# Second attention rebuilt: head pairs on two row halves, pair-wide maxima and exponentials, x-hat and y's low part on GpSimd, new task orders

## The reference

```
# block 0: one head of 256 channels, scale 1/16
h = film(rmsnorm(x, norm1_w), cond);  Q, K, V = h @ q_w + q_b, h @ k_w + k_b, h @ v_w + v_b
x = x + softmax(Q K^T / 16) V @ proj_w + proj_b
x = x + gelu(film(rmsnorm(x, norm2_w), cond) @ mlp_w1 + mlp_b1) @ mlp_w2 + mlp_b2
# block 1: 16 heads of 16 channels, modulated by six rows of silu(c) @ w_ada + b_ada
xm = layernorm(x) * (1 + scale_msa) + shift_msa
k, q, v = split(xm @ w_qkv, 3);  q = q / 16                 # heads (256, 16, 16)
y = softmax(q k^T over keys) v;  x = x + gate_msa * (y @ w_proj + b_proj)
xm = layernorm(x) * (1 + scale_mlp) + shift_mlp
x = x + gate_mlp * (gelu_tanh(xm @ w_mlp1 + b_mlp1) @ w_mlp2 + b_mlp2)
```

## Time and profile before

| | us |
|---|---|
| median of 3 runs | 1827.96 (1824.01 to 1829.28) |
| span of the profiled execution | 1819.8 |
| median run less that span | 8.2 |
| TensorE busy | 1757.5 (97%) |
| VectorE busy | 1340.7 (74%) |
| ScalarE busy | 944.7 (52%) |
| GpSimd busy | 362.4 (20%) |

### The profile page before, as it was taken

The page is one execution under the profiler, slowest core; times in us unless marked ns, Lnnn a source line. Parts: engine busy times, 40 slices in busy tenths (PEclk is TensorE's granted clock), DMA queues, the critical chain, the costliest instruction groups (busy, mean ns, idle before and its releaser), DMA issues. The chain is left out here.

```text
span 1819.8 us, 46726 instructions
## 1 busy us (share of the span) xinstructions
PE 1757.5 (97%) x15198; PEld 1633.4 (90%) x15198; DVE 1340.7 (74%) x3119; ACT 944.7 (52%) x2099; POOL 362.4 (20%) x470
## 2 busy tenths in 40 slices
PE   7999989999999969999999999999998899999998
PEld 7999989999999967888888888888886899999998
DVE  4888876666666647888888888888885677777776
ACT  2666653333333345777676777777776333333332
POOL 2233331222122200111111111111111212221221
PEclk8999989999999989999999999999999799999999
DMA  7300010000000002111111111111110111111111
GB/s 215 127 20 20 20 33 1 0 0 0 0 0 0 0 14 72 52 49 50 48 48 48 48 48 48 48 48 49 49 49 27 50 47 46 35 46 46 46 42 39
DMA packets 73579, 73.97 MB, mean 41 GB/s; under 512 B 13489, under 2 KB 63985, under 8 KB 73537
## 3 DMA queue, kind: packets, MB, share of 16 engines
q1 hardware_dynamic: 70928, 73.31, 12.9%
q10 hardware_dynamic: 2448, 0.08, 0.1%
q0 software_dynamic: 160, 0.04, 0.0%
HBM read 38.62 MB, written 8.55 MB: 26 GB/s over the span
## 5 line engine op out<-in xcount | busy, mean ns | idle before, releaser
L1418 DVE TENSOR_REDUCE C_negmax<-bank 128x2 f32<-128x512 f32 x512 | 340.2, 686 | 101.1 <-PE bank L1226 98.1
L1338 ACT ACTIVATE C_probs<-bank 128x512 f32<-128x512 f32 x512 | 301.3, 598 | 139.2 <-PE bank L1238 134.4
L1226 PE MATMUL bank<-C_kx,C_qs 128*128 128x256 f32 x1024 | 217.9, 295 | 5.1 <-DMA C_kx<-C_k_hi 2.6
L892 ACT ACTIVATE D_g<-bank,D_bias 128x256 f32<-128x256 f32 x256 | 107.6, 472 | 221.3 <-PE bank L181 221.3
L1238 PE MATMUL bank<-C_qs,C_kx 128*128 128x256 f32 x1024 | 221.2, 298 | 0.1
L892 ACT ACTIVATE B_g<-bank,B_bias 128x256 f32<-128x256 f32 x256 | 107.6, 472 | 218.5 <-PE bank L181 193.1
L1226 PEld LDWEIGHTS bank<-C_kx,C_qs 128*128 128x128 f32 x1024 | 156.2, 189 | 33.3 <-issue 17.7
L1238 PEld LDWEIGHTS bank<-C_qs,C_kx 128*128 128x128 f32 x1024 | 155.9, 189 | 29.0 <-ACT C_probs L1338 15.6
L181 PE MATMUL bank<-D_wt_w_hi,D_g_lo 128*128 128x256 f32 x512 | 147.3, 288 | 6.0 <-DVE D_g_lo L920 4.6
L181 PE MATMUL bank<-B_wt_w_hi,B_g_lo 128*128 128x256 f32 x512 | 145.7, 285 | 5.2 <-DVE B_g_lo L920 5.0
L181 PE MATMUL bank<-B_h_hi,B_wt_w_lo 128*128 128x256 f32 x512 | 147.4, 288 | 1.9 <-DVE B_h_lo L294 1.9
(11 more groups left out here) (265 smaller groups left out, 5218.0 us busy)
## 6 DMA issues: line engine op xcount, KB each, us to landing
C_kx<-C_k_hi SPq DMA_DIRECT2D x256, 64.0 KB, 2.6
C_kx<-C_k_lo SPq DMA_DIRECT2D x128, 64.0 KB, 2.6
C_gbc<-mod_rows SPq DMA_DIRECT2D x32, 256.0 KB, 3.2
D_gbc<-mod_rows SPq DMA_DIRECT2D x32, 256.0 KB, 3.4
out<-xres SPq DMA_DIRECT2D x32, 256.0 KB, 3.5
xres<-in_x SPq DMA_DIRECT2D x4, 1792.0 KB, 16.6
A_orow_bc<-mod_rows SPq DMA_DIRECT2D x32, 128.0 KB, 2.9
stage<-in_L_cond_mlp_w SPq DMA_DIRECT2D x2, 1024.0 KB, 12.5
```

Source lines behind the costliest of these rows:

```text
L892: ins = eng.activation(g[u][:, d * S:(d + 1) * S], hbank[u][:, d * S:(d + 1) * S], func, bias=per_seq(bias1, 2 * u + d, b))
L1226: ins = eng.matmul(sbank[h % 2][:, qh * S:(qh + 1) * S], qs[b.par][:, t * S + qh * P:t * S + (qh + 1) * P], kx[b.par][e][:, t * S:(t + 1) ...
L1338: e_exp.by(eng.activation(probs[h % NP][:, :], stbank[h % 2][:, :], ACT.Exp, scale=scl))
L1418: e_max.by(eng.tensor_reduce(n3[:, :, col], sbank[h % 2][:, :].rearrange("p (q k) -> p q k", q=TH), AX, ALU.max, negate=True))
```

## The change

In the second attention:

- `kx` has one tile per parity instead of two; a pair's heads use rows 0 to 63 and 64 to 127 of `qs` and `kx` as two separate 64-row products. Stacks are interleaved with step 4: row 4c + slot. Slots 0 to 2 hold q hi, hi, lo and k lo, hi, hi; slot 3 holds the maxima's hi and lo (rows 3, 35, 67, 99).
- `w_q` is permuted in the preamble as `w_k` was, so that one DMA per part fills half of a stack (`place`, three of 128 KB for q, three for k, in each half of the heads). A DMA of zeros clears the maxima's rows (`clear`), one DMA brings them (`place_max`). `SQ0` to `SQ3`, `sel` and the copies on ScalarE go.
- Scores, maxima and exponentials work on a pair: 4 matmuls into two adjacent banks, one reduction and one exponential over 1024 elements. There is one such two-bank tile for scores and one for transposed scores; the next pair waits until it is read.
- The maxima are split before their transposition (`ms0`, `ms1` on VectorE), so one copy (`mc0`, `mc1` on ScalarE) evacuates them.
- `xhat` moves from VectorE to GpSimd, as two subtractions and two multiplications with a broadcast operand. `lo_y` moves there too and reads a copy `y_f` that ScalarE makes.
- The tables of times are new, `MAX_SKEW` is 5 instead of 3, `PEEL` 6 instead of 4.

```diff
-PEEL = 4
+PEEL = 6
+X_FIRST = 4
...
-        banks = [ps(f"bank{i}", [P, 512]) for i in range(8)]
+        bank_pairs = [ps(f"bank{i}", [P, 1024]) for i in range(4)]
+        banks = [pair[:, half:half + 512] for pair in bank_pairs for half in (0, 512)]
...
-        SLOTS, MAX_SKEW = 16, 3
+        SLOTS, MAX_SKEW = 16, 5
...
@@ normalize
+                if eng is nc.gpsimd:
+                    for h in range(TH):
+                        mean = self.mv[:, 2 * h:2 * h + 1].broadcast_to([P, D])
+                        ins = eng.tensor_tensor(self.xhat[:, h * D:(h + 1) * D], x_at(b)[:, h], mean, ALU.subtract)
+                    self.e_xc.by(ins)
+                    self.e_xc.wait(eng, b)
+                    for h in range(TH):
+                        o = self.xhat[:, h * D:(h + 1) * D]
+                        ins = eng.tensor_tensor(o, o, self.rstd[:, h:h + 1].broadcast_to([P, D]), ALU.mult)
+                    self.e_xhat.by(ins)
+                    return
...
+                T_PE = {"T": 13.95, "q": 19.19, "k": 22.91, "v": 30.82, "S0": 36.65, "S1": 38.63, "S2": 40.35, "S3": 42.23,
+                        "S4": 44.34, "M0": 44.60, "S5": 46.32, "S6": 48.27, "ST0": 48.53, "ST1": 50.21, "S7": 50.48,
+                        "ST2": 51.89, "M1": 52.90, "AV0": 53.07, "ST3": 53.99, "ST4": 57.03, "AV1": 57.29, "ST5": 58.71,
+                        "Y1a": 59.94, "ST6": 60.77, "AV2": 61.02, "ST7": 62.56, "AV3": 64.80, "Y1b": 66.80, "Y2": 70.26,
+                        "PR": 74.49}
+                T_ACT = {"hi_h": 16.05, "hi_q": 22.12, "hi_k": 24.84, "vout": 35.67, "mc0": 45.03, "exp0": 49.07,
+                         "exp1": 50.75, "exp2": 52.43, "mc1": 53.39, "exp3": 55.89, "exp4": 57.57, "Y0": 58.50,
+                         "exp5": 59.25, "exp6": 61.36, "exp7": 63.10, "Y1": 66.01, "hi_y": 70.89}
+                T_DVE = {"stats": 0.00, "lo_h": 18.19, "lo_q": 24.12, "lo_k": 26.00, "max0": 37.30, "max1": 39.02,
+                         "max2": 40.89, "max3": 42.78, "ms0": 44.11, "max4": 44.98, "max5": 46.86, "max6": 49.05,
+                         "max7": 51.02, "ms1": 52.36, "nY1a": 62.12, "nY1b": 68.61, "out": 76.30}
+                T_POOL = {"root": 1.26, "xhat": 4.13, "xb": 50.49, "lo_y": 72.18, "res": 77.28}
+                T_SP = {"z0": 22.53, "q0": 25.41, "k0": 27.33, "z1": 31.10, "q1": 33.98, "k1": 35.92, "md0": 45.53,
+                        "gates": 47.82, "md1": 53.92}
+                BANK = {"T": 2, "q": 2, "k": 0, "v": 1, "M0": 2, "M1": 1, "Y1a": 0, "Y1b": 0, "Y2": 1, "PR": 1}
...
+                        def scores(b, t):
+                            w = t // 4
+                            if t % 4 == 0:
+                                eng.wait_ge(s_qd[w][b.par], (b.pair + 1) * Q_DMAS * 16)
+                                eng.wait_ge(s_kd[w][b.par], (b.pair + 1) * K_DMAS * 16)
+                            e_max.wait(eng, b, t)
                             for qh in range(TH):
-                                ins = eng.matmul(sbank[h % 2][:, qh * S:(qh + 1) * S],
-                                                 qs[b.par][:, t * S + qh * P:t * S + (qh + 1) * P],
-                                                 kx[b.par][e][:, t * S:(t + 1) * S], start=True, stop=True)
-                            e_s.by(ins)
+                                for e in range(2):
+                                    rows = slice(e * HALF, (e + 1) * HALF)
+                                    ins = eng.matmul(spair[:, (e * TH + qh) * S:(e * TH + qh + 1) * S],
+                                                     qs[b.par][rows, t * S + qh * P:t * S + (qh + 1) * P],
+                                                     kx[b.par][rows, t * S:(t + 1) * S], start=True, stop=True)
+                                    if qh == TH - 1:
+                                        e_s.by(ins)
...
+                            e_exp.by(eng.activation(probs[t % NP][:, :], stpair[:, :], ACT.Exp, scale=scl))
...
+                            e_yf.by(eng.activation(y_f[:, :], mbank("Y2")[:, :], ACT.Copy))
...
+                            e_max.by(eng.tensor_reduce(m4[:, :, :, j], spair[:, :].rearrange("p (e q k) -> p e q k", e=2, q=TH),
                                                        AX, ALU.max, negate=True))
...
+                        def place(b, w, name, stacked, slots, e_lo, landed):
+                            e_lo.wait(eng, b)
+                            for slot, part in enumerate(slots):
+                                eng.dma_start(half(stacked, b, w, slot), qk[name + part][:, w * S:(w + 1) * S].bitcast(F32))\
+                                   .then_inc(landed[w][b.par], 16)
```

More of the change, by code:

```diff
@@ L1171, in phase_l1_attention @@
                 scl = 1.0 / CH
-                T_PE = {"T": -0.5, "q": 3, "k": 6.5, "v": 16.5, "SQ0": 8.5, "SQ1": 12, "SQ2": 13, "SQ3": 14.5,
-                        "M0": 25.5, "M1": 33, "AV0": 38, "AV1": 41, "AV2": 46.5, "AV3": 49.5, "Y1a": 45, "Y1b": 52,
-                        "Y2": 55, "PR": 59}
-                T_ACT = {"hi_h": 0.5, "hi_q": 3.5, "hi_k": 6.5, "v": 18, "SQ0": 8, "SQ1": 12.5, "SQ2": 14,
-                         "SQ3": 15.5, "M0": 25.5, "M1": 32.5, "Y0": 42, "Y1": 50, "hi_y": 56}
@@ L1179, in phase_l1_attention @@
-                T_DVE = {"stats": -3.5, "xhat": -2, "lo_h": 1.5, "lo_q": 4.5, "lo_k": 7.5, "M0": 26, "M1": 33.5,
-                         "Y1a": 46, "Y1b": 53.5, "lo_y": 57, "out": 59.5}
-                EARLY = 4
-                T_S, T_ST = {h: 16 + h for h in range(NH)}, {h: 32.5 + h for h in range(NH)}
-                pe_order = schedule(EARLY, T_S, {f"ST{h}": t for h, t in T_ST.items()}, T_PE)
-                ring = [(k, n) for k, n in pe_order if n in T_PE and not n.startswith("AV")]
-                names = [n for _, n in ring]
@@ L1190, in mbank @@
[L1190 to L1197 removed]
+                PAIRS = range(NT)
@@ new lines, in scores_t @@
+                        def scores_t(b, t):
+                            w = t // 4
+                            if t % 4 == 0:
+                                eng.wait_ge(s_md[w][b.par], (b.pair + 1) * 16)
+                            e_exp.wait(eng, b, t)
+                            for kh in range(TH):
+                                for e in range(2):
+                                    rows = slice(e * HALF, (e + 1) * HALF)
+                                    ins = eng.matmul(stpair[:, (e * TH + kh) * S:(e * TH + kh + 1) * S],
+                                                     kx[b.par][rows, t * S + kh * P:t * S + (kh + 1) * P],
+                                                     qs[b.par][rows, t * S:(t + 1) * S], start=True, stop=True)
+                                    if kh == TH - 1:
+                                        e_st.by(ins)
@@ L1474, in _ @@
-                        for h in range(NH):
-                            tasks[h] = lambda b, h=h: maximum(b, h)
-                        run_tasks(eng, schedule(EARLY, T_S, T_DVE), tasks)
+                                 "lo_k": lambda b: lo_bias(b, "k", qk["k_hi"], qk["k_lo"], bias_k, e_hik, e_lok),
+                                 "ms0": lambda b: max_split(b, 0), "ms1": lambda b: max_split(b, 1),
+                                 "nY1a": lambda b: y_norm(b, 0), "nY1b": lambda b: y_norm(b, 1), "out": gated}
@@ new lines, in residual @@
+                        def residual(b):
+                            e_xb.wait(eng, b)
+                            e_tmp.wait(eng, b)
+                            for h in range(TH):
+                                ins = eng.tensor_tensor(xn[:, b.num, h], xn[:, b.num, h], tmp[:, h * D:(h + 1) * D], ALU.add)
+                            e_res.by(ins)
+                        run_tasks(eng, schedule(0, T_POOL), {
+                            "root": lambda b: norm.root(eng, b), "xhat": lambda b: norm.normalize(eng, b),
+                            "lo_y": lo_y, "xb": add_bias, "res": residual})
```

386 lines of the change are left out of this document (157 added, 229 removed).

## The result

The changed kernel takes 1745.5 us (median of 4 runs, 1742.1 to 1751.8) against 1828.6 for the kernel before (4 runs, 1824.0 to 1831.1): a ratio of 0.9555, 95% interval 0.9532 to 0.9578. The forecast was 1706, so the sign and the range were right and the size was not: 83 us came instead of 122.

What follows compares the result with a forecast made beforehand. TensorE was taken to bound the kernel: 17.98 us of work plus 0.5 of waits, period 18.5. Stage 32 x 18.5 + 35.5 + 1.2 = 628.7 instead of 750.7, so 1827.96 -> 1706 us; range 1664 to 1775.

Steps and rivals of the forecast that it cites:

- Fill and drain: Filling and draining the second attention's pipeline, with skew of five slots: 35.5 us, from 25 to 55, against 33.3 before.
- The 8.2 that I put between span and median: Added to the forecast profiled span of 1698 us to get the median run, 1706.
- 24 changes 2.28: TensorE's changes of array division per period: 24 at 0.095 us each, 2.28 us; the old order had 8.
- the 0.08 that I charged behind each of four transposes: TensorE, per period: the two matmuls behind each four transposes take 0.08 us more than 0.24; transposes total 1.72.
- the likeliest case: Second attention's period of 18.5 us, own range 17.8 to 19.3, giving 1684 to 1732 us; chance 0.55.
- the 0.5 of waits: TensorE's waits per period, with pairs filling both score banks: 0.5 us instead of 0.27.
- Free changes: Rival: changes of division cost nothing for row halves; period 17.0 or 16.7 us, time 1648 to 1658; chance 0.12.
- No overlap: Rival: row halves run serially, 0.24 us more per score task; time 1821, or 1773 without changes; chance 0.14.
- the estimate of 1802: Within the rival of unoverlapped halves: four serial weight loads make a score task 0.43 us, the time 1802.
- Slower: Rival: in 64-row mode loads can't run ahead of matmuls; 0.94 us per score task, period 29.7, time 2064; chance 0.05.
- The chain of waits: Rival: score task, maximum and signals in turn set the period, 20.4 us, time 1767; chance 0.12.
- GpSimd's part: X-hat and y's low part on GpSimd: 4.5 us more a period, 8.1, at most 11.1, hidden behind TensorE.

Runs made afterwards that it cites:

- merged_exp3: merged_order with ScalarE's fourth exponential placed ahead of the two copies of y instead of behind them: 1724.5 us, ratio 0.9446.
- st0_first: merged_exp3 with one transposed-score task (ST0) ahead of score task S6 in TensorE's order instead of behind it: 1727.0 us, ratio 0.9471.
- merged_exp3_init: merged_exp3 with ScalarE's second filling of the zero and one rows moved behind the first sequence's k copy: 1731.2 us, ratio 0.9486.
- on_vector: The changed kernel with x-hat and y's low part back on VectorE instead of GpSimd: 1759.2 us, ratio 0.9643.
- merged_order: The changed kernel with three entries of TensorE's order moved so score tasks adjoin, 19 changes of division instead of 24: 1743.0 us, ratio 0.9550.

## Why the prediction was right in direction and 39 us off

**Where the 39 us are.** 32 periods x (19.68 - 18.5) = 37.8. Fill and drain 40.1 against 35.5: 4.6. The preamble from the last result of the stage before to the first statistics took 10.1 against 7.1 + 1.2 = 8.3: 1.8. That makes a span of 1698 + 44.2 = 1742.2, and with the 2.0 that the changed kernel's profiled run lies above its span 1744, against 1745.5. The 8.2 that I put between span and median was mostly chance of the one profiled execution of before: every run on record is only 1.7 to 2.3 above its own span.

**The step that failed** is the term "24 changes 2.28" of the new TensorE sum: 0.095 each, "the only measured one". The rows were read correctly, 0.19 for two changes, but around an `AV` group, and I carried this to row halves while writing that the new ones cost "between 0 and 0.095". The upper bound was wrong: 0.095 is not a bound from above, because in those rows one side of the changes lies inside the group's own 1.00. The trace of before has it: in all its 89 whole `AV` groups of the middle, the matmuls begin in fours 0.24, 0.22 and 0.22 apart, and the next task begins 0.33 behind the last four, 0.11 more than the step between fours. Eight changes by themselves cost 0.195 each. The period fits: 16 new changes x 0.095 more = 1.52, less 0.3, makes the 1.2 that was missing, 18.5 + 1.2 = 19.7. The 0.3 is most likely the 0.08 that I charged behind each of four transposes, where it falls together with a change; that was not tested by itself. The Trainium skill says ("TensorEngine Tiling (Array Packing)", Key Properties) that a change of tiling mode drains the engine. The traces agree: behind `k` the next weight load begins only 0.32 after the one before (1010.53 to 1010.85), together with its matmul.

**Luck in the range.** 1745.5 lies outside the 1684 to 1732 that I gave the likeliest case. It is inside 1664 to 1775 only because that range made room for rivals, and none of them is what happened.

**Fill and drain** were 4.6 above the forecast, and why stays open. They were 39.5 at a period of 19.10 (merged_exp3) and 47.1 and 47.2 at 21.24 and 20.88, which looks like five slots of skew that grow with the period. But 42.8 at 19.08 (st0_first), 43.3 at 19.10 (merged_exp3_init) and 40.2 at 20.16 (on_vector) don't follow such a line.

**What held.** Score tasks run in 0.24, their matmuls starting in pairs within 0.02 us, and in 0.47 without the halves. Maxima, exponentials, ScalarE, DMA share and the 0.5 of waits came as costed; GpSimd and VectorE within their bounds. TensorE stayed the bound.

**The rivals.** Free changes: refuted, by twice what I had charged. No overlap: refuted by the 0.24; the estimate of 1802 from the Trainium skill ("TensorE: Matmul & The Clock Gate", LDWEIGHTS) falls with it, since it ran four loads one after the other, while here four loads of two halves take 0.30 together. Slower, by loads that can't run ahead: refuted, for the loads of S2 and ST4 are done by 1011.38 and their eight matmuls begin by 1011.32. The chain of waits, 20.4 a period, did not set this kernel's period of 19.68, though its terms of 0.2 and 0.1 for ends and signals had no row behind them (ST1 starts 0.05 behind the end of its exponential). It is next in line: merged_order took five changes away and got 0.18 of 0.8, and in merged_exp3 ST6 still waits 0.17 for an exponential.

**What I called hidden and was not.** GpSimd's part was forecast to cost nothing, and it cost nothing; but I credited nothing to it either. Undone, it costs 13.6 us, through y's low part alone: I had compared VectorE's busy time with TensorE's and not asked what stands ahead of each maximum.

## What to carry to other kernels

When tasks of different array divisions alternate, price every change by a pair of full-width tasks with one divided task between them, on both sides of each start, and not by a group that may hide one side; then sort the order to have few changes. After each reordering look at the in-order queue that frees the shared bank: one exponential behind two copies ate 0.40 of the 0.58 us that five changes fewer gave. Before you shorten a wait, ask whether it lies inside a longer chain to the next task: ST1's did. Slack of an engine in its sum is no cover for an operation placed ahead of the one that the bound engine waits for.

## What the runs showed of the hardware

A change between the full array and a 64-row half cost TensorE 0.19 to 0.20 us: the last matmul ahead of it took 0.09 more to the next start, the first one behind it 0.10 more. Behind a single 64-row matmul between full-width ones both fall into one gap, 0.31 instead of 0.12. Two row halves gave the full factor of two (0.24 against 0.47 for four matmuls of 256 columns). And the order in which a task named its halves was free: matmuls began in twos in both orders, in the period of 19.68 and 19.73. The Trainium skill says ("TensorE: Matmul & The Clock Gate", Step-by-step: what each phase is for) that matmuls stay in program order and only loads are pulled ahead. In the kernel that names each half twice in a row, the matmul named third began ahead of the one named second in all 512 score tasks, which speaks against that for matmuls on different row halves, unless the order was changed before it reached the chip.
